# Layer 2 of a two-layer cross attention: where ScalarE rounds a batch's fourth fetched block, and the order of work in the first and last head

## The reference

```
# layer 1 (one head): layer norm of x and context, then
q = qn @ Wq.T + bq;  k = kvn @ Wk.T + bk;  v = kvn @ Wv.T + bv
x = x + (softmax(q @ k.T) @ v) @ Wd.T + bd
# layer 2 (8 heads of 256), context not normed, mask all ones
Q, K, V = x @ Wq, ctx @ Wk, ctx @ Wv        # per head
ctx_h = softmax(where(mask, Q @ K.T / 16, -inf)) @ V
out = concat(ctx_h) @ Wo + x
return layer_norm(out) * gamma + beta
```

## Time and profile before

| what | value |
|---|---|
| time, median of 3 (lowest, highest) | 520.58 us (520.45, 520.63) |
| the profiled execution, its span | 522.14 us, 520.3 us |
| busy: PE, DVE, ACT, POOL | 480.1, 337.3, 288.3, 242.0 us |
| share of the span: PE, DVE, ACT, POOL | 92%, 65%, 55%, 47% |
| spill, issue to landing (neg_scores, probs) | 3.1, 3.5 us |
| fetch part of 128 KB, issue to landing | 3.0 us |
| head 0, a middle head | from about 82 us, 50.6 us each |

### The profile page before, as it was taken

The page is one execution under the profiler, slowest core; times in us unless marked ns, Lnnn a source line. Parts: engine busy times, 40 slices in busy tenths (PEclk is TensorE's granted clock), DMA queues, the critical chain, the costliest instruction groups (busy, mean ns, idle before and its releaser), DMA issues.

```text
span 520.3 us, 7533 instructions
## 1 busy us (share of the span) xinstructions
PE 480.1 (92%) x2424; PEld 396.6 (76%) x2424; DVE 337.3 (65%) x681; ACT 288.3 (55%) x465; POOL 242.0 (47%) x136
## 2 busy tenths in 40 slices
PE   1989999997999999999999999999999999898992
PEld 0867787775878887888788878888888888677892
DVE  5999774664575657565755576567656665775357
ACT  4676475556465656565656565565656564635222
POOL 4646565438635353535354535454453533533004
PEclk9999999998999999999999999999999999999997
DMA  8413023847675664475548564765566546541002
GB/s 265 130 42 122 1 61 122 237 158 238 169 231 163 202 202 164 160 227 176 194 134 250 174 205 138 237 190 173 164 199 201 173 153 192 190 139 42 0 2 81
DMA packets 53974, 81.97 MB, mean 158 GB/s; under 512 B 5792, under 2 KB 43072, under 8 KB 53824
## 3 DMA queue, kind: packets, MB, share of 16 engines
q1 hardware_dynamic: 44992, 50.16, 33.9%
q10 hardware_dynamic: 8960, 31.54, 15.6%
HBM read 49.16 MB, written 32.51 MB: 157 GB/s over the span
## 4 chain that ended last, share of the span: by engine, by line
PE 60%; DVE 16%; ACT 9%; issue 8%; POOL 3%; DMA 2%; ACTq 1%; DVEq 0%; SPq 0%; POOLq 0%
PE ps_scores L594 21%; PE ps_o L616 5%; PE ps_o L617 4%; PE ps_o L618 4%; PE ps_o L620 4%; PE ps_o L619 4%; DVE probs L1300 3%; ACT o_hi L990 2%; PE ps_task L544 2%; PE ps_task L542 2%; PE ps_task L543 2%; DVE o_lo L1318 2%; ACT probs L952 2%; ACT o_lo L992 2%; DMA ctx_raw<-in_context 2%
## 5 line engine op out<-in xcount | busy, mean ns | idle before, releaser
L489 POOL TENSOR_TENSOR probs_t_lo<-probs_t_lo,probs_t_hi 128x1024 fp32r<-128x1024 f32 x60 | 144.0, 2401 | 197.8 <-ACT probs_t_hi L962 197.8
L616 PE MATMUL ps_o<-probs_t_hi,val_hi 128*128 128x512 f32 (+1 forms) x144 | 58.8, 408 | 6.5 <-DVE o_lo L1318 4.8
L962 ACT ACTIVATE probs_t_hi<-probs_t_lo 128x1024 fp32r<-128x1024 f32 x60 | 62.8, 1046 | 1.5 <-DMA probs_t_lo<-scratch 1.5
L1263 DVE RECIPROCAL row_inv<-row_sum 128x1 f32<-128x1 f32 x72 | 11.2, 158 | 74.0 <-PE ps_scores L594 67.4
L618 PE MATMUL ps_o<-probs_t_hi,val_lo 128*128 128x512 f32 (+1 forms) x144 | 56.9, 395 | 0.0
L617 PE MATMUL ps_o<-probs_t_lo,val_hi 128*128 128x512 f32 (+1 forms) x144 | 56.8, 395 | 0.0
L619 PE MATMUL ps_o<-probs_t_hi,val_rem 128*128 128x512 f32 (+1 forms) x144 | 56.7, 394 | 0.0
L620 PE MATMUL ps_o<-probs_t_lo,val_rem 128*128 128x512 f32 (+1 forms) x144 | 56.7, 394 | 0.0
L1300 DVE STREAM_TRANSPOSE probs<-probs 128x1024 f32<-128x1024 f32 x30 | 37.3, 1245 | 25.9 <-ACT probs L952 25.9
L594 PE MATMUL ps_scores<-key_hi,q_hi 128*128 128x512 f32 x144 | 46.5, 404 | 3.0 <-DVE neg_scores L1276 1.7
L952 ACT ACTIVATE probs<-probs,row_min 128x1024 f32<-128x1024 f32 x30 | 34.5, 1151 | 22.2 <-DVE row_min L1293 22.2
(11 more groups left out here) (247 smaller groups left out, 1095.2 us busy)
## 6 DMA issues: line engine op xcount, KB each, us to landing
probs_t_lo<-scratch SPq DMA_DIRECT2D x240, 128.0 KB, 3.0
scratch<-neg_scores ACTq DMA_DIRECT2D x30, 512.0 KB, 3.1
scratch<-probs ACTq DMA_DIRECT2D x30, 512.0 KB, 3.5
ring<-in_weights_a SPq DMA_DIRECT2D x9, 512.0 KB, 5.5
ring<-in_weights_b SPq DMA_DIRECT2D x9, 512.0 KB, 4.8
ring<-in_keys_t SPq DMA_DIRECT2D x4, 512.0 KB, 3.4
ctx_raw<-in_context SPq DMA_DIRECT2D x2, 768.0 KB, 9.3
ring<-in_context SPq DMA_DIRECT2D x16, 96.0 KB, 2.5
```

Source lines behind the costliest of these rows:

```text
L489: nc.gpsimd.tensor_tensor(pt_lo[b][:, t, :, :], pt_lo[b][:, t, :, :].bitcast(f32), pt_hi[b][:, t, :, :].bitcast(f32), ALU.subtract).then_i ...
L616: pe.matmul(o0, val_hi[b][:, kt, :], hi, start=first, stop=False)
L962: act.activation(pt_hi[b][:, t, :, :], pt_lo[b][:, t, :, :].bitcast(f32), ACT.Copy)\
```

## The change

In ACT's loop body the `round_moved` of the fourth block of a batch (block 3 of this head at j = 5, block 7 of the head before at j = 1) goes from behind `exp` to the head of the block. In the first head ACT rounds blocks 1, 2 and 3 at the head of j = 3, 4 and 5, queries of task 0 and the remainder of task 5 go ahead of exp, `w_hi` of piece B1 behind the spill of j = 3, and the spill of j = 1 ahead of `round_outputs`; DVE splits task 5 before its transpose. In the last head ACT rounds the weights at j = 3 and not j = 2, POOL splits block 0 before these weights, and at j = 5 ACT and DVE take the probabilities of block 4 before the outputs. Nothing that is computed changes.

```diff
--- before.py
+++ after.py
@@ -508,12 +508,12 @@
                         split_weights(2 * h + (HI_OF[PC_V11] - 1), 1)
                     if j == 4 and not last_head:
                         split_weights(2 * h + HI_OF[PC_V11], 0)
-                    if j == 2 and last_head:
-                        split_weights(2 * h + (HI_OF[PC_V11] - 1), 0)
                     if j < 2:
                         split_moved(h - 1, j + 6)
                     else:
                         split_moved(h, j - 2)
+                    if j == 2 and last_head:
+                        split_weights(2 * h + (HI_OF[PC_V11] - 1), 0)
 
             with pool.Fori(1, HEADS - 1) as h:
                 body(h)
@@ -1163,6 +1163,14 @@
                 for j in range(2 * QT):
                     if j == 3:
                         round_y(1)
+                        round_moved(0, 1)
+                        round_queries(task_no(0, 0), 1, 0, 1)
+                    if j == 4:
+                        round_moved(0, 2)
+                        round_values(PC_V10, 1, (0,))
+                    if j == 5:
+                        round_moved(0, 3)
+                        move_remainder(task_no(0, 5), 0)
                     if j == 6:
                         round_folded(task_no(0, 5), 0)
                     exp(0, j)
@@ -1170,24 +1178,24 @@
                         round_keys(PC_KA1, 1)
                     if j == 1:
                         round_weights(ring_count(PC_A2), 1)
+                        spill(0, 1)
                         round_outputs(-1, 1)
                     if j == 3:
-                        round_queries(task_no(0, 0), 1, 0, 1)
                         round_queries(task_no(0, 1), 1, 1, 1)
                         round_a(task_no(0, 2), 0, -1.0 / 16, CTX)
                         round_a(task_no(0, 3), 1, -1.0 / 16, CTX)
-                        round_weights(ring_count(PC_B1), 0)
                     if j == 4:
                         round_queries(task_no(0, 4), 0, 0, 1)
-                    if j == 5:
-                        move_remainder(task_no(0, 5), 0)
                     if j >= 6:
                         keep_b(task_no(0, j), j - 6)
-                    if j >= 2:
+                    if j == 2 or j >= 6:
                         round_moved(0, j - 2)
-                    spill(0, j)
-                    if j in (4, 6):
-                        round_values(PC_V10, 1, (j // 2 - 2,))
+                    if j != 1:
+                        spill(0, j)
+                    if j == 3:
+                        round_weights(ring_count(PC_B1), 0)
+                    if j == 6:
+                        round_values(PC_V10, 1, (1,))
 
             def body(h):
                 last_head = isinstance(h, int) and h == HEADS - 1
@@ -1196,7 +1204,9 @@
                     if j == 0 and not last_head:
                         act.wait_ge(task_done, task_no(h, 0))
                         round_weights(16 * h + (ring_count(PC_V11 + 1) - 16), 1)
-                    if j == (2 if last_head else 4):
+                    if j % QT == 1:
+                        round_moved(h - 1 if j < 2 else h, (j + 6) % (2 * QT))
+                    if j == (3 if last_head else 4):
 
                         act.wait_ge(task_done, TASKS0 + 8 * h + 2 if last_head else task_no(h, 4))
                         round_weights(16 * h + (ring_count(PC_V11 + 2) - 16), 0)
@@ -1222,9 +1232,11 @@
                                 act.wait_ge(b_split, h)
                             keep_b(task, j - 6)
                     exp(h, j)
-                    if j < 2:
-                        round_moved(h - 1, j + 6)
-                    elif not (last_head and j >= 6):
+                    if last_head and j == 5:
+                        round_probs(h, 4)
+                    if j == 0:
+                        round_moved(h - 1, 6)
+                    elif j % QT != 1 and not (last_head and j >= 6):
                         round_moved(h, j - 2)
                     if not (last_head and j >= QT):
                         spill(h, j)
@@ -1232,8 +1244,6 @@
                         round_outputs(h - 1, 0)
                     if j == 5:
                         round_outputs(h - 1, 1)
-                        if last_head:
-                            round_probs(h, 4)
 
             first_body()
             with act.Fori(1, HEADS - 1) as h:
@@ -1587,13 +1597,15 @@
                     if j == 3:
                         split_task(0, 0)
                         split_task(0, 1)
+                    if j == 5:
+                        split_task(0, j)
                     turn_blocks(0, j)
                     if j == 1:
                         split_outputs(-1, 1)
                     if j == 3:
                         split_task(0, 2)
                         split_task(0, 3)
-                    if j in (4, 5):
+                    if j == 4:
                         split_task(0, j)
                     if j == 6:
                         split_folded(0, 0)
@@ -1624,9 +1636,9 @@
                     if j == 1:
                         split_outputs(h - 1, 0)
                     if j == 5:
-                        split_outputs(h - 1, 1)
                         if last_head:
                             split_probs(h, 4)
+                        split_outputs(h - 1, 1)
 
             first_body()
             body(1)
```

## The result

The changed kernel takes 521.9 us in the median of 20 runs (520.5 to 525.0), the kernel before 520.74 (520.03 to 522.03): ratio 1.0025, 95% interval 1.0014 to 1.0037. It is 1.2 us slower where 4.9 us faster was forecast, and outside the range of 514.0 to 518.9. The profiled execution has a span of 520.7 (522.48 us in all) beside 520.3 before.

| start of head | before | after | after less before |
|---|---|---|---|
| 0 | 84.2 | 84.0 | -0.2 |
| 1 | 136.2 | 131.9 | -4.3 |
| 2 | 186.1 | 190.0 | +3.9 |
| 7 | 438.8 | 442.6 | +3.8 |
| end of the span | 520.3 | 520.7 | +0.4 |

The account below looks back on a forecast made before the run. PE's own work was taken as the bound, with gaps to win only in head 0 and the last head. 4.0 - 1.45 - 0.1 + 2.8 - 0.4 = 4.85 us took the median 520.58 to 515.7; 8-in-10 range 514.0 to 518.9.

Parts of the forecast that it names:

- Head 0, rounding earlier: Head 0: two PE gaps (second before block 6's values) shrink by 2.1 us, overlap 0.3, full clock 1.6; 4.0 won.
- Heads 1 to 7: Rounding before exp waits for late block 7 in head 1; 1.45 us lost, PE's wait 0.85 becoming 2.3.
- The clock as a rival: Head 1's 2.3 us wait brings the lower clock, ten value matmuls cost 1.6 us more: 517.3; chance 15%.
- The middle heads: Heads between head 1 and the last: rounding fits ACT's idle time; 0.1 us lost for all of them.
- the 0.2 to spare: Head 4 to 5: block 7's fetch lands at 343.7 against 344.98, leaving 0.2 us beyond the rounding.
- Last head: Two edits of the last head win 2.8 us, less 0.4 for a late fetch going into it.
- (a): Last head, weights rounded at j=3, POOL splitting block 0 first: PE's 1.44 us wait before `project` goes but for 0.1; 1.3 won.
- (b): Last head at j=5, rounding before exp, probabilities before outputs: PE's whole 1.46 us wait before block 5's transposes goes.
- The 0.4 for a late block 7: Into the last head: block 7's fetch lands at 445.5, too late for the earlier rounding; 0.4 us lost.
- Five sixths of the span is PE's own work: Whole kernel: PE is busy almost throughout the middle heads, so the change can win only where PE has gaps.
- The rival on the slower side: ACT waits for the fetch at the head of block 1 in every head, before `move_remainder`: 523.0; chance 7%.
- The collision in head 0: DVE's folded split at j=6 meets POOL's split of block 4, stands 2.4 us; 2.75 won, 517.8; chance 20%.

Follow-up runs that it names:

- e9: Kernel before with one edit of the last head: weights rounded at block 3, POOL's split of block 0 before them; 518.8 us, ratio 0.996.
- e12: Changed kernel with SP issuing head 1's first weights at block 4 of head 0, not block 5; 520.0 us, ratio 0.9977.
- e7: Changed kernel with four memory buffers for spilled tiles, not two, and the spill ahead of the rounding in blocks 6 and 7 of head 0; 521.5 us.
- e10: e6 with SP issuing head 1's first weights at block 4 of head 0, not block 5; 514.92 us, ratio 0.9881.
- e2: Kernel before with only the loop body's move of fourth-block rounding to the head of blocks 1 and 5; 526.4 us, ratio 1.0099.
- e5: Changed kernel with 9 and 12 extra matmuls in PE's two waits of head 1; 521.13 us, ratio 1.0005.
- e1: Changed kernel with ACT's rounding of block 7 of head 0 put back behind exp in head 1 alone; 518.29 us, ratio 0.9947.
- e6: Kernel before with the edits of head 0 and of the last head, no move in the loop body; 517.98 us, ratio 0.9938.
- e4: Kernel before with the last head's edits alone (weights, POOL's split order, probabilities before outputs); 517.12 us, ratio 0.9933.

## Why the prediction was wrong, step by step

- *Head 0, rounding earlier: 4.0.* Right in mechanism and in the profile (4.1). Mis-sized against the median: 1.6 of it was the lower clock behind the second gap, which the profiled execution before had (522.14) and most runs have not. In the 16 runs beside e9 to e12 the kernel before took 520.5 to 520.9 at a granted clock of 0.992 to 0.994 and 521.7 to 522.2 at 0.990 or 0.991, six of 16. So the gain against the median was about 2.5.
- *Heads 1 to 7: "The change shifts both alike, so here the chain slips 0.5 + 1.05", 1.45 in the sum.* This is the step that failed. PE came 4.3 us earlier, the landing of block 7 did not: 143.38 after, 143.5 before. In the changed kernel the spills and fetches of blocks 5 to 7 follow each other at the pace of the DMA engines. Their share was high from 126 to 134 in both kernels (0.87 before, 0.91 after); before, block 7's spill came behind that, at 134.7, and took 3.5 us, now it comes into it at 131.6 and takes 5.9. Of the 4.3 us, 1.2 went before this spill was issued, where ACT stood until 131.54 for an earlier fetch, 2.4 in the spill and 0.6 in the last part of the fetch (4.6 us instead of 4.0). e7 and e10 speak for the load, and not the time of issue, setting the landing. So `rem_sum` slipped by 5.9 us, not by 1.45, PE waited 5.0 us more, and with the clock head 1 lost 8.2 where 1.45 stands in the sum. Where PE was not earlier (e2), the wait was right: 2.57 measured, 2.3 forecast.
- *The clock as a rival, 1.6 us at 15%.* It came, and larger, since the waits were 2.5 and 3.3 us in a row. e5 puts its cost at 2.4 in the profile and 0.8 between the medians. That PE's recent activity sets it, as the Trainium skill has it ("TensorE: Matmul & The Clock Gate", section "What's actually happening"), agrees with these rows: 0.50 behind 5.85 us of waits, 1.00 in e10 behind 1.16. Between these the outcome was open: 1.00 behind 2.43 in e1's profile, 0.50 behind 2.57 in e6's. A wait of 2.3 had the lower clock in two profiles of three (e2 and e6, not e1), so 15% was low.
- *The middle heads, 0.1.* Right in this profile (3.2 us of waits after, 3.1 before). e2's has 0.70 in head 5, so the 0.2 to spare that I read from one landing was no margin.
- *Last head, 2.8 less 0.4.* Right in mechanism, and undersized: 3.4 in the profile, 3.8 in e4. (a) gave 2.0 against 1.3. In e9's profile PE gets from its value product of block 1 to the transposes 1.8 us sooner; 1.6 of it is the wait of 1.44 with the overlap that it broke, for which the prediction took 1.3. (b) the 1.46 went. The 0.4 for a late block 7 did not come: PE's wait before that product is 0.89 in both profiles.
- *"Five sixths of the span is PE's own work."* The rows do not give this figure: the stretch read, 160 to 440, is 280 of 520 us. No term of the sum hangs on it.
- *The rival on the slower side* put the waits in all heads at 7%. The place was right, `fetched` before `move_remainder`, but one head sufficed, with a slip four times as long.
- *The collision in head 0* did not come: the folded split ran 126.07 to 126.71, ahead of POOL at 126.64.

## What to carry to other kernels

When an engine is made earlier, ask of every transfer that it will meet whether its landing moves too: measure the pace of the DMA chain by itself, and do not carry a margin read behind the old gap over to the new order. A wait for a DMA should not stand on an in-order engine ahead of the work that the bound engine needs next, even if it fits an idle time in the profile. And look for the transfer that can move into a half idle stretch before adding buffers.

## What the runs showed of the hardware

A spill issued 0.6 us earlier into engines under load landed 0.4 us later (6.9 us in flight instead of 5.9, one trace each, e7 and the changed kernel). One and the same kernel ran at a lower granted clock in some runs and not in others: before the change in two groups, 1.4 us apart, and in e6 spread over 6 us from 0.995 to 0.987. A wait of PE of 2.43 us was followed by full clock (e1), one of 2.57 by 3.4 us at half clock (e6), each in one profiled run. One profiled execution does not tell which group a term belongs to; the three times ahead of the prediction, all 1.5 us below the profiled one, did.
